# Rotated keys of the cross attention: two of four blocks multiplied in pieces among the self attention's last exponentials, GpSimd adding and halving them, query blocks ahead of the last keys

## The chip, the cores and the metric

The kernel runs on one core of one Trainium2 chip. A core has TensorE (PE, matrix products; its weight loads are shown as PEld), VectorE (DVE), ScalarE (ACT), GpSimd (POOL) and SyncE (SP, which issues DMAs). They run side by side, each through its own queue in the order of the program, and wait for each other on semaphores. The metric is the device time of one execution in microseconds (us), lower is better. TensorE's clock has two levels, 2.4 and 1.2 GHz; the profile shows the granted share as 1.00 and 0.50.

## The reference, cut to what matters

A decoder of two layers on `x` (4, 512, 256) with a context (4, 1024, 256): windowed attention, attention with latents, a ternary feed forward, self attention, cross attention with rotary positions, and a routed feed forward of eight experts. Each is added to `x` behind a layer norm. The change is in the cross attention, whose keys and values come from the raw context:

```python
q = proj(query, Wq, bq, Lq)          # 16 heads of 16; query = layernorm(x), 512 rows
k = proj(key, Wk, bk, Lk)            # key = ctx_1024, 1024 rows
v = proj(value, Wv, bv, Lk)
q = apply_rope(q, q_cos, q_sin)      # (x1 c - x2 s, x1 s + x2 c)
k = apply_rope(k, k_cos, k_sin)
scores = jnp.einsum('bhqd,bhkd->bhqk', q, k) * scale
attn = jax.nn.softmax(scores, axis=-1)
out = jnp.einsum('bhqk,bhkd->bhqd', attn, v)
```

## The kernel before, in words

The kernel goes through the four batch elements one after the other, and in each through the six stages. A product of float32 quality is made of float16 halves: each operand is a high and a low half, and `product` adds high x high, high x low and low x high (L574, L575, L576) over the two chunks of the 256 contracted rows. A product of 128 x 512 thus takes six matrix instructions.

*Rotation.* Six blocks of 128 rows (eight heads) by 512 columns (tokens) are rotated, numbered j: j = 0 to 3 are the keys (feature half j // 2, token half j % 2), j = 4 and 5 the queries. `rope_product(b, j)` makes two products for a block, one with the weights and one with weights whose halves of a head are swapped (s_ = 0, 1). `rotate(b, j)` on VectorE adds the biases and multiplies by the tables of cosines and sines (L1841, two instructions of about 0.74 us). The two results are added (L500 on GpSimd for j < 4, L1849 on VectorE for the queries), ScalarE makes the high half (L1352) and VectorE the low half (L1855). Blocks j = 0 and 1 are multiplied in the tail of the self attention, the others at the beginning of the cross attention, the queries last, for they need the norm of `x`.

*Selection.* `select_k` and `select_q` (L953) spread four heads of a block to rows that start at multiples of 64, by products with a table of zeros and ones; ScalarE copies them (L1365, L1370; the first query tile by VectorE, L1900). There are eight such tiles (p_ = 0 to 7).

*Attention* (`attend`, m_ = 0 for self, 1 for cross). First every score is made once with queries on the rows, in *slots* a = 0, 1, ... (L865, two instructions), and VectorE takes the negated maxima (L1793); a slot reads two of the banks 0 to 3. Four groups of four heads each get their shift (L875, L1807, L1808), which a DMA puts beside the queries. Then the scores are made again with keys on the rows (L897, two per *half step*), ScalarE takes the exponentials (L1340), and `weigh` multiplies them with the values (L911). After a group's last, ScalarE copies the output (L1331), TensorE transposes it (L921), VectorE divides (L1824, L1826). Self attention has 32 slots and 16 steps of two half steps, numbered 0 to 31; the slots run ahead of the steps and end at half step 19. In the first 13 (self) or 21 (cross) slots nothing of the steps runs yet, and `between_self` and `between_cross` put selections and value products (`cross_value`) between the slots.

*Tail.* After the last step: the last L921, `rope_product(b, 0)`, the transpose of the divided output (L628), `rope_product(b, 1)`, ScalarE's and VectorE's halves of it (L1185, L1542), the output projection (L583 to L587, then L574 to L576 of 256 columns), and its additions to `x` with the statistics of the next norm (L1885, L1463). Then the cross attention begins: variance (L1477), reciprocal root on GpSimd (L550), normalised rows (L1483), their transposes (L601) and halves (L1187, L1544). `keep_warm(n, bank)` (L594) issues n products without use.

The order of all this is written out by hand on every engine; on TensorE the lines of `cross_attention(b)` are the blocks j = 2 and 3, transposes, `keep_warm(8, 2)`, blocks 4 and 5, the first selections, `attend(b, 1)`.

## Time and profile before

| | |
|---|---|
| median of 3 runs | 2313.86 us (2306.58 to 2318.06) |
| the profiled execution | 2310.29 us, its span 2308.5 us |
| TensorE busy (matrix products) | 2029.1 us, 88% |
| VectorE | 1771.6 us, 77% |
| ScalarE | 1340.6 us, 58% |
| GpSimd | 205.1 us, 9% |
| chain that ended last | PE 52%, DVE 27%, DMA 8%, issue 6%, ACT 5% |
| mean granted clock of TensorE | 0.978 |

A batch takes about 565 us. The stretch of the change in the first one lies between 409 and 471 us from the start of the span. "Busy" of TensorE counts the modelled end of each product, so what tells of its pace is the distance of starts. A row of the timeline gives the start and length of a group in us, the engine, the line, what it writes and reads, and in brackets how long the engine was idle before it and what ended that.

### The profile page before, as it was taken

To read this page: it belongs to the slowest core of one execution; us is meant where nothing else is said; L and a number is where in the kernel's file an instruction comes from. 1 tells how busy PE (TensorE), PEld (TensorE's weight loads), DVE (VectorE), ACT (ScalarE), POOL (GpSimd) and SP (SyncE) were. 2 spreads that over 40 slices of the span, in tenths; PEclk is the share of its full clock that TensorE was granted. 3 is DMA by queue.
4 is the path that set the end of the run, shared out by engine and by line. 5 is a ranking of instruction groups with operands and counts; after the bars stand their busy time and mean duration, and the time that the engine had idled before them with its cause. 6 is when DMAs were issued, how large, how long until landed. Compare 5 with 4: busy or idle time off the path is not lost.

```text
span 2308.5 us, 43343 instructions
## 1 busy us (share of the span) xinstructions
PE 2029.1 (88%) x18074; PEld 1142.4 (49%) x18074; DVE 1771.6 (77%) x2755; ACT 1340.6 (58%) x1993; POOL 205.1 (9%) x211
## 2 busy tenths in 40 slices
PE   2899978988989996998899998798998999779898
PEld 1566743323656763242466666333255776433235
DVE  7787878695778867779587786769958888786956
ACT  3566636577356654748636664474844666355682
POOL 2000001141000000114000000101500000011220
PEclk9999989999999998999999999899999999999999
DMA  6276720010047670002006775001001766300100
GB/s 253 44 124 118 130 44 1 1 74 29 19 73 123 125 122 19 2 1 93 11 19 106 120 122 113 0 2 69 25 10 36 124 124 120 75 1 1 74 2 10
DMA packets 417315, 147.68 MB, mean 64 GB/s; under 512 B 404440, under 2 KB 412768, under 8 KB 416224
## 3 DMA queue, kind: packets, MB, share of 16 engines
q1 hardware_dynamic: 416544, 142.82, 30.1%
q8 instruction: 142, 2.33, 0.4%
q0 software_dynamic: 576, 2.10, 0.3%
q14 instruction: 53, 0.43, 0.1%
HBM read 41.86 MB, written 2.10 MB: 19 GB/s over the span
## 4 chain that ended last, share of the span: by engine, by line
PE 52%; DVE 27%; DMA 8%; issue 6%; ACT 5%; POOL 1%; SPq 1%; POOLq 0%; DVEq 0%; ACTq 0%
DVE nmx L1793 10%; PE ps L574 10%; PE ps L576 9%; PE ps L575 9%; DMA arena<-arena 7%; PE ps L911 4%; PE ps L736 3%; DVE arena L1632 3%; PE ps L953 2%; PE ps L897 2%; PE ps L730 2%; PE ps L731 2%; PE ps L594 2%; PE ps L865 2%; DVE arena L1737 1%
## 5 line engine op out<-in xcount | busy, mean ns | idle before, releaser
L1793 DVE TENSOR_REDUCE nmx<-ps 128x2 f32<-128x1024 f32 x384 | 444.0, 1217 | 22.1 <-PE ps L865 20.4
L1340 ACT ACTIVATE arena<-ps 128x512 f32<-128x512 f32 x768 | 405.3, 602 | 55.0 <-PE ps L897 50.2
L574 PE MATMUL ps<-arena 128*128 128x512 f16 (+1 forms) x800 | 273.4, 342 | 3.5 <-DVE arena L1933 2.7
L575 PE MATMUL ps<-arena 128*128 128x512 f16 (+1 forms) x800 | 273.2, 341 | 0.0
L576 PE MATMUL ps<-arena 128*128 128x512 f16 (+1 forms) x800 | 273.0, 341 | 0.0
L1619 DVE TENSOR_SCALAR_CACHE_REDUCE ps<-ps 128x1536 f32<-128x1536 f32 x128 | 225.8, 1764 | 54.1 <-PE ps L576 53.5
L911 PE MATMUL ps<-arena 128*17 128x256 f32 x3072 | 237.8, 385 | 0.0
L1632 DVE SCALAR_TENSOR_TENSOR arena<-arena,rs 128x1536 f16<-128x1536 f32 x128 | 231.5, 1809 | 4.2 <-ACT arena L1245 4.2
L1245 ACT ACTIVATE arena<-arena,rs 128x1536 f16<-128x1536 f32 x128 | 200.8, 1568 | 40.1 <-DVE rs L1625 40.1
L1238 ACT ACTIVATE arena<-ps,nm 128x1536 f32<-128x1536 f32 x128 | 197.1, 1540 | 19.5 <-DVE ps L1619 19.5
L730 PE MATMUL ps<-arena 128*128 128x128 f16 x1536 | 185.3, 219 | 3.3 <-DMA arena<-arena 3.1
L731 PE MATMUL ps<-arena 128*128 128x128 f16 x1536 | 185.3, 219 | 0.0
L897 PE MATMUL ps<-arena 64*128 64x512 f16 x768 | 172.6, 387 | 14.3 <-DMA arena<-arena 10.2
L865 PE MATMUL ps<-arena 64*128 64x512 f16 x768 | 148.7, 385 | 17.7 <-DVE nmx L1793 9.4
L574 PE MATMUL ps<-wh,arena 128*128 128x128 f16 (+2 forms) x856 | 154.9, 223 | 6.5 <-DVE arena L1555 6.5
L730 PEld LDWEIGHTS ps<-arena 128*128 128x128 f16 x1536 | 150.2, 98 | 11.9 <-DMA arena<-arena 4.4
L575 PE MATMUL ps<-wl,arena 128*128 128x128 f16 (+2 forms) x856 | 154.6, 223 | 0.0
L576 PE MATMUL ps<-wh,arena 128*128 128x128 f16 (+2 forms) x856 | 154.5, 223 | 0.0
L731 PEld LDWEIGHTS ps<-arena 128*128 128x128 f16 x1536 | 150.3, 98 | 7.5
L550 POOL TENSOR_TENSOR rstd<-ve,col 128x4 f32<-128x4 f32 x20 | 20.2, 1010 | 1408.4 <-DVE ve L1477 1238.5
L897 PEld LDWEIGHTS ps<-arena 64*128 64x128 f16 x768 | 48.1, 92 | 181.3 <-ACT arena L1340 136.3
L736 PE MATMUL ps<-arena 128*128 128x128 f16 x1536 | 108.3, 221 | 29.2 <-DMA arena<-arena 29.1
(254 smaller groups left out, 3855.8 us busy)
## 6 DMA issues: line engine op xcount, KB each, us to landing
arena<-in_experts SPq DMA_DIRECT2D x4, 3840.0 KB, 11.7
arena<-in_weights SPq DMA_DIRECT2D x8, 929.0 KB, 12.6
arena<-in_ctx SPq DMA_DIRECT2D x4, 1024.0 KB, 5.3
arena<-arena SPq DMA_TRANSPOSE x256, 3.7
arena<-in_ctx_t SPq DMA_DIRECT2D x4, 1024.0 KB, 4.8
arena<-in_ternary SPq DMA_DIRECT2D x2, 1024.0 KB, 5.9
y<-in_x POOLq DMA_DIRECT2D x4, 512.0 KB, 4.2
x<-in_x SPq DMA_DIRECT2D x4, 512.0 KB, 3.8
```

The costliest lines, as they stand in the source:

```text
L574: mm(out_, lh, rh, start=(k == 0), stop=False)
L575: mm(out_, lh, rl_, start=False, stop=False)
L576: last = mm(out_, ll, rh, start=False, stop=(k == n - 1))
L730: mm(d_, vh[:, kt, :], ph[:, kt, :], start=(kt == 0), stop=False)
L731: mm(d_, vl[:, kt, :], ph[:, kt, :], start=False, stop=False)
L897: mm(ps[:, 4 + n % 3, :], ks[rows, 2 * g_ + pp, P * kt:P * kt + P], qs[rows, 2 * g_ + pp, :], start=True, stop=True).then_inc(b_mm.sem, 1)
L911: mm(ps[32 * j:32 * j + VW, 7, cols], v17[:, kt, 4 * g_ + j, :], pr_[:, (4 * t + j) % RING, cols], start=(kt + half == 0), stop=(kt == mod ...
L1245: A(xq[i % 2][0], xp[:, i % 2, :], ACT.Copy, scale=rs[:, i:i + 1]).then_inc(s_hi.sem, 1)
L1340: A(pr_[:, n % RING, :], ps[:, 4 + n % 3, :], ACT.Exp).then_inc(b_exp.sem, 1)
L1619: TS_(s_, s_, -XS, None, ALU.mult, ALU.min, accum_out=nm[:, i:i + 1]).then_inc(s_max.sem, 1)
L1632: STT(xq[i % 2][1], xp[:, i % 2, :], rs[:, i:i + 1], xq[i % 2][0], ALU.mult, ALU.subtract).then_inc(s_lo.sem, 1)
L1793: V.tensor_reduce(nmx[:, g_ % 2, ch, :, pp, i], ps[:, 2 * (z % 2):2 * (z % 2) + 2, :], AX.X, ALU.max, negate=True)\
```

## The change

Each block is now handled in parts: `rope_part(b, j, s_)` is one of its two products, and `rotate(b, j, s_)` one of the two instructions on VectorE. `RP_PARTS` is the order.

- Blocks 0 and 1 (four products, 24 instructions) leave the tail. `early_rope` issues them from half step 22 of the self attention on: two instructions in front of each `weigh` up to half step 31, then one in front of each of the last four. They write banks 1 and 3. VectorE rotates block 0 in steps 12 and 13 and block 1 ahead of the last output.
- GpSimd adds and makes both halves of all key blocks and of the second query block (`turned`); ScalarE's and VectorE's halves of them go. The first query block keeps VectorE for the sum and the low half, ScalarE for the high half.
- The cross attention begins with one product of block 2, the first selection of keys, the other product of block 2; then the transposes of the normed rows, both products of block 4, and the first products of blocks 3 and 5. The second products of 5 and 3 come behind the slots 0 and 1, as do their rotations. `keep_warm(8, 2)` goes.
- Value products 0 to 3 stood behind the slots 1, 2, 5, 6 and stand behind 2, 4, 5, 6.
- `rt` gets a third room (8 KB to 12 KB per partition).

TensorE, self attention of the first batch, from the L897 pair of half step 28. Before (L897 scores, L921 transposes of the output, L911 weighing, L628 transposes of `y`):

```order
L897 MATMUL ps<-arena 128x512 x2
L921 MATMUL ps<-ident,arena 128x128 x4
L911 MATMUL ps<-arena 17x256 x4
L897 MATMUL ps<-arena 128x512 x2
L911 MATMUL ps<-arena 17x256 x4
L628 MATMUL ps<-ident,y 128x128 x4
L897 MATMUL ps<-arena 128x512 x2
```

Of the change (L927, L951, L941, L658 are the same four, L1103 the key products):

```order
L927 MATMUL ps<-arena 128x512 x2
L951 MATMUL ps<-ident,arena 128x128 x4
L1103 MATMUL ps<-arena,wh 128x512 x2
L941 MATMUL ps<-arena 17x256 x4
L927 MATMUL ps<-arena 128x512 x2
L1103 MATMUL ps<-arena,wl 128x512
L1103 MATMUL ps<-arena,wh 128x512
L941 MATMUL ps<-arena 17x256 x4
L658 MATMUL ps<-ident,y 128x128 x4
L927 MATMUL ps<-arena 128x512 x2
```

Two key products stand ahead of each weighing. At the end of the same stage, before (12 key products, L574 to L576, stand between L921 and L628):

```order
L911 MATMUL ps<-arena 17x256 x20
L921 MATMUL ps<-ident,arena 128x128 x4
L574 MATMUL ps<-arena,wh 128x512
L575 MATMUL ps<-arena,wh 128x512
L576 MATMUL ps<-arena,wl 128x512
```

Of the change (L613 is the first product of the output projection):

```order
L941 MATMUL ps<-arena 17x256 x4
L1103 MATMUL ps<-arena,wl 128x512
L941 MATMUL ps<-arena 17x256 x4
L1103 MATMUL ps<-arena,wh 128x512
L941 MATMUL ps<-arena 17x256 x4
L1103 MATMUL ps<-arena,wh 128x512
L941 MATMUL ps<-arena 17x256 x4
L1103 MATMUL ps<-arena,wl 128x512
L941 MATMUL ps<-arena 17x256 x4
L951 MATMUL ps<-ident,arena 128x128 x4
L658 MATMUL ps<-ident,y 128x128 x4
L613 MATMUL ps<-wh,yT_hi 128x256
```

The last five weighings are parted by four single products, and the tail has none. VectorE from the halves of the normed rows to the first slots of the cross attention, before (L1841 rotations, L1855 low halves, L1849 sums, L1900 first query tile, L1793 maxima):

```order
L1544 TENSOR_TENSOR yT_lo<-ps,yT_hi 128x512 x2
L1841 SCALAR_TENSOR_TENSOR arena<-ps,col,rope_k 128x512 x2
L1855 TENSOR_TENSOR arena<-arena 128x512
L1841 SCALAR_TENSOR_TENSOR arena<-ps,col,rope_q 128x512 x2
L1849 TENSOR_TENSOR arena<-arena 128x512
L1855 TENSOR_TENSOR arena<-arena 128x512
L1841 SCALAR_TENSOR_TENSOR arena<-ps,col,rope_q 128x512 x2
L1855 TENSOR_TENSOR arena<-arena 128x512
L1849 TENSOR_TENSOR arena<-arena 128x512
L1900 TENSOR_SCALAR arena<-ps 128x512
L1793 TENSOR_REDUCE nmx<-ps 128x2
L1855 TENSOR_TENSOR arena<-arena 128x512
```

Of the change (L1594, L1890, L1897, L1901, L1951 and L1843 for L1544, L1841, L1849, L1855, L1900 and L1793):

```order
L1594 TENSOR_TENSOR yT_lo<-ps,yT_hi 128x512 x2
L1890 SCALAR_TENSOR_TENSOR arena<-ps,col,rope_q 128x512 x2
L1897 TENSOR_TENSOR arena<-arena 128x512
L1890 SCALAR_TENSOR_TENSOR arena<-ps,col,rope_k 128x512
L1901 TENSOR_TENSOR arena<-arena 128x512
L1890 SCALAR_TENSOR_TENSOR arena<-ps,col,rope_q 128x512
L1951 TENSOR_SCALAR arena<-ps 128x512
L1843 TENSOR_REDUCE nmx<-ps 128x2
L1890 SCALAR_TENSOR_TENSOR arena<-ps,col,rope_q 128x512
L1843 TENSOR_REDUCE nmx<-ps 128x2
L1890 SCALAR_TENSOR_TENSOR arena<-ps,col,rope_k 128x512
L1843 TENSOR_REDUCE nmx<-ps 128x2 x14
```

One low half of six is left, and two rotations have moved behind the slots.

The diff, cut to its core:

```diff
+        RP_PARTS = ((0, 0), (0, 1), (1, 0), (1, 1), (2, 0), (2, 1), (4, 0), (4, 1), (3, 0), (5, 0), (5, 1), (3, 1))
+        RP_BANK = dict(zip(RP_PARTS, (1, 3, 1, 3, 6, 7, 4, 5, 6, 7, 7, 7)))
+        RP_ROOM = (0, 1, 0, 1, 2, 0)
+        RP_POOL = (0, 1, 2, 5, 3)
+        EARLY_ROPE = 22
...
-        CROSS_SELECT, CROSS_VALUE = (3, 7, 11, 12, 14, 15, 16), (1, 2, 5, 6, 9, 10, 18, 19)
+        CROSS_SELECT, CROSS_VALUE = (3, 7, 11, 12, 14, 15, 16), (2, 4, 5, 6, 9, 10, 18, 19)
...
+            def turned(b, j):
+
+
+                n, r_ = RP_POOL.index(j), rt[:, RP_ROOM[j]]
+                pool.wait_ge(rp_mul.sem, rp_mul.at(b, rp_upto(j, 1)))
+                nc.gpsimd.tensor_tensor(r_[:, 0, :], r_[:, 0, :], r_[:, 1, :], ALU.add).then_inc(rp_sum.sem, 1)
+                if j == 0:
+                    pool.wait_ge(sel_mm.sem, sel_mm.at(b, LH))
+                pool.wait_ge(rp_sum.sem, rp_sum.at(b, n + 1))
+                nc.gpsimd.tensor_copy(rp_dest(j, 0), r_[:, 0, :]).then_inc(rp_hi.sem, 1)
+                pool.wait_ge(rp_hi.sem, rp_hi.at(b, n + 1))
+                nc.gpsimd.tensor_tensor(rp_dest(j, 1), r_[:, 0, :], rp_dest(j, 0), ALU.subtract).then_inc(rp_lo.sem, 1)
...
                 for k in range(5):
                     if k == 3:
-                        add_rotated(b, 0)
+                        turned(b, 0)
+                        turned(b, 1)
                     pool.wait_ge(var_ready.sem, var_ready.at(b, k + 1))
...
                     if k == 3:
-                        for j in range(1, 4):
-                            add_rotated(b, j)
+                        for j in RP_POOL[2:]:
+                            turned(b, j)
...
                     pe.wait_ge(lv_hi.sem, lv_hi.at(b, 2 + i // 2))
+                elif i == 0:
+                    pe.wait_ge(rp_mul.sem, rp_mul.at(b, 12))
...
 
             def between_cross(b, a):
 
-                if a in CROSS_SELECT:
+                if a == 0:
+                    rope_part(b, 5, 1)
+                elif a == 1:
+                    rope_part(b, 3, 1)
...
                             output_slot(b, mode, mode.output_after(2 * t + half))
+                        if m_ == 0 and 2 * t + half == EARLY_ROPE:
+                            pe.wait_ge(cr_lo.sem, cr_lo.at(b, DC))
+                            pe.wait_ge(sl_free.sem, sl_free.at(b, mode.slot0 + mode.z_shift[GROUPS - 1] + 1))
+                        if m_ == 0 and 2 * t + half >= EARLY_ROPE:
+                            early_rope(b, 2 * (2 * t + half - EARLY_ROPE), 2)
                         if t >= 2:
...
                 for t in range(mode.steps - 2, mode.steps):
                     for half in range(2):
+                        if m_ == 0:
+                            early_rope(b, 20 + 2 * (t - mode.steps + 2) + half, 1)
                         weigh(b, mode, t, half)
                 output_slot(b, mode, GROUPS - 1)
+                pe.wait_ge(y_ready.sem, y_ready.at(b, Y_FIRST[3 + 2 * m_] + 1))
                 if m_ == 0:
-                    pe.wait_ge(cr_lo.sem, cr_lo.at(b, DC))
-                    rope_product(b, 0)
-                pe.wait_ge(y_ready.sem, y_ready.at(b, Y_FIRST[3 + 2 * m_] + 1))
+                    pe.wait_ge(rp_mul.sem, rp_mul.at(b, 4))
                 transpose_chunk(1, 1)
-                if m_ == 0:
-                    rope_product(b, 1)
...
+            def rope_part(b, j, s_, first=0, n=3 * DC):
+
+
+                at = RP_PARTS.index((j, s_))
+                bank, m = RP_BANK[j, s_], rp_source(j)
+                if first == 0:
+                    if at in (2, 3):
+                        pe.wait_ge(rp_mul.sem, rp_mul.at(b, at - 1))
+                    elif at >= 8:
+                        pe.wait_ge(rp_mul.sem, rp_mul.at(b, {8: 5, 9: 6, 10: 10, 11: 11}[at]))
+                name = (("ck", "cks"), ("cq", "cqs"))[j // 4][s_]
+                src = [both(yT, slice(None), c) if j >= 4 else both(crT, slice(None), c, slice(512 * (j % 2), 512 * (j % 2) + 512))
+                       for c in range(DC)]
+                pairs = [(W(name, c, P * m, P), src[c]) for c in range(DC)]
+                if (j, s_) == (4, 0):
+                    last = first_product(b, 4, ps[:, bank, :], pairs, False)
+                else:
+                    for k in range(first, first + n):
+                        (lh, ll), (rh, rl_) = pairs[k // 3]
+                        last = mm(ps[:, bank, :], ll if k % 3 == 2 else lh, rl_ if k % 3 == 1 else rh,
+                                  start=(k == 0), stop=(k == 3 * DC - 1))
+                if first + n == 3 * DC:
+                    last.then_inc(rp_mm.sem, 1)
+
+            def early_rope(b, k, n):
+
+
+                for at in range(k, k + n):
+                    rope_part(b, *RP_PARTS[at // 6], at % 6, 1)
 
             def cross_attention(b):
-                for j in range(2, 6):
-                    if j == 4:
-                        transpose_y(b, 4)
-                        keep_warm(8, 2)
-                    rope_product(b, j)
+                rope_part(b, 2, 0)
+                select_k(b, 1, 0)
+                rope_part(b, 2, 1)
+                transpose_y(b, 4)
+                pe.wait_ge(k_st.sem, k_st.at(b, LH // 2 + 1))
+                for j, s_ in ((4, 0), (4, 1), (3, 0), (5, 0)):
+                    rope_part(b, j, s_)
                 pe.wait_ge(lx_added.sem, lx_added.at(b, NT))
-                select_k(b, 1, 0)
                 select_q(b, 1, 0)
                 attend(b, 1)
...
             def cross_attention(b):
+                stacked_k(b, 1, 0)
                 split_hi(b, 4, yT)
-                for j in range(2, 5):
-                    rotated_hi(b, j)
-                stacked_k(b, 1, 0)
-                rotated_hi(b, 5)
+                first_q_hi(b)
                 for p_ in range(1, 8):
                     if p_ < 4:
                         values_hi(b, 1 + p_, p_ - 1, 7)
...
+            def rotate(b, j, s_):
+
+
+                n = rp_upto(j, s_)
+                dve.wait_ge(rp_mm.sem, rp_mm.at(b, n))
+                if s_ == 0 and j in (2, 3, 5):
+                    dve.wait_ge(rp_lo.sem, rp_lo.at(b, {2: 1, 3: 2, 5: 3}[j]))
+                m, t0 = rp_source(j), 512 * (j % 2)
...
+                name = (("cbk", "cbks"), ("cbq", "cbqs"))[j // 4][s_]
+                STT(rt[:, RP_ROOM[j], s_, :], ps[:, RP_BANK[j, s_], :], C(name, m), tab[:, s_, :], ALU.add, ALU.mult)\
+                    .then_inc(rp_mul.sem, 1)
...
                     slots(b, mode, a, a + 1)
                     if m_ == 0 and a < 2:
                         self_lo(b, 2 + a)
-                    elif m_ == 1 and a == 0:
-                        rotated_lo(b, 5)
...
+                        rotate(b, 0, 1)
                 add_rows(("sbo", "cbo")[m_])
+                if m_ == 0:
+                    rotate(b, 1, 0)
+                    rotate(b, 1, 1)
                 outputs(b, mode, GROUPS - 1)
                 split_lo(b, 3 + 2 * m_, yT, bias=("sbv", "cbv")[m_])
-                if m_ == 0:
-                    rotate(b, 0)
...
 
             def cross_attention(b):
                 moments(b, 3, x, NT)
-                rotate(b, 1)
-                rotated_lo(b, 0)
+                rotate(b, 2, 0)
                 normalise(b, 3, x, y)
-                rotated_lo(b, 1)
-                rotate(b, 2)
+                rotate(b, 2, 1)
                 split_lo(b, 4, yT)
-                rotate(b, 3)
-                rotated_lo(b, 2)
-                rotate(b, 4)
-                rotate_sum(b, 4)
-                rotated_lo(b, 3)
-                rotate(b, 5)
-                rotated_lo(b, 4)
-                rotate_sum(b, 5)
+                rotate(b, 4, 0)
+                rotate(b, 4, 1)
+                first_q_sum(b)
+                rotate(b, 3, 0)
+                first_q_lo(b)
+                rotate(b, 5, 0)
                 first_q(b, 1)
```

## Rows read from the trace of the kernel before

**Rows 1.** Stretches: their ends, length, busy (count) by engine, granted clock, DMA, GB/s.
```profile
427.31:436.01 8.70, 8.70 (x57) 5.60 (x58) 4.94 (x11) 1.32 (x2) 1.27 (x1) 1.00 0.00 1
454.10:459.74 5.64, 5.64 (x28) 2.39 (x26) 5.22 (x6) 1.39 (x2) 0.00 (x0) 0.70 0.00 0
```

**Rows 2.** Timeline of TensorE in the last exponentials: start, us, group [idle before].
```profile
412.53 0.58 PE L897 MATMUL ps<-arena 64*128 64x512 f16 x2
...
415.01 0.39 PE L897 MATMUL ps<-arena 64*128 64x512 f16 x2 [0.37 <-DMA arena<-arena]
...
418.92 0.49 PE L897 MATMUL ps<-arena 64*128 64x512 f16 x2
...
420.10 0.63 PE L921 MATMUL ps<-ident,arena 128*128 128x128 f32 x4 [0.68 <-ACT arena L1331]
...
421.21 0.39 PE L897 MATMUL ps<-arena 64*128 64x512 f16 x2
421.53 0.63 PE L911 MATMUL ps<-arena 128*17 128x256 f32 x8
422.09 0.66 PE L628 MATMUL ps<-ident,y 128*128 128x128 f32 x4
422.68 0.39 PE L897 MATMUL ps<-arena 64*128 64x512 f16 x2
...
424.07 2.35 PE L911 MATMUL ps<-arena 128*17 128x256 f32 x40
427.31 0.63 PE L921 MATMUL ps<-ident,arena 128*128 128x128 f32 x4 [0.89 <-ACT arena L1331]
```

**Rows 3.** Timeline of ScalarE, an exponential and the halves of the normed rows.
```profile
421.63 1.09 ACT L1340 ACTIVATE arena<-ps 128x512 f32<-128x512 f32 x2 [0.70 <-PE ps L897]
...
442.84 1.08 ACT L1187 ACTIVATE yT_hi<-ps 128x512 f16<-128x512 f32 x2 [1.24 <-PE ps L601]
```

**Rows 4.** Timeline of VectorE from the norm to the maxima.
```profile
437.74 0.17 DVE L1477 TENSOR_SCALAR ve<-mv 128x4 f32<-128x4 f32 x1
...
439.74 2.32 DVE L1483 TENSOR_SCALAR y<-x,mv,rstd 128x256 f32<-128x256 f32 x4
...
443.90 1.27 DVE L1544 TENSOR_TENSOR yT_lo<-ps,yT_hi 128x512 f16<-128x512 f32 x2
...
452.82 0.69 DVE L1900 TENSOR_SCALAR arena<-ps 128x512 f16<-128x512 f32 x1
...
459.74 10.42 DVE L1793 TENSOR_REDUCE nmx<-ps 128x2 f32<-128x1024 f32 x9 [0.41 <-PE ps L865]
```

**Rows 5.** Timeline of TensorE from the transposes to slot 0 of the cross attention.
```profile
442.75 1.89 PE L594 MATMUL ps<-wh,ident 128*128 128x512 f16 x8
444.48 0.38 PE L583 MATMUL ps<-yT_hi,wh 128*128 128x512 f16 x1
...
452.18 0.60 PE L953 MATMUL ps<-arena,sel 128*128 128x512 f16 x2 [1.49 <-DVE arena L1855]
453.66 0.61 PE L865 MATMUL ps<-arena 64*128 64x512 f16 x4 [0.88 <-DVE arena L1900]
```

**Rows 6.** Stretches: the cross attention's tail in batches 0 and 1 (columns of Rows 1).
```profile
560.88:567.79 6.91, 5.44 (x33) 3.66 (x34) 3.73 (x9) 0.69 (x1) 0.00 (x0) 0.75 0.00 0
1122.05:1127.89 5.84, 4.09 (x33) 3.07 (x34) 3.63 (x9) 0.69 (x1) 0.00 (x0) 1.00 0.01 3
```

**Rows 7.** GpSimd by line: shapes, count, busy us, mean ns, idle before.
```profile
L521 POOL TENSOR_TENSOR arena<-arena 128x512 f16<-128x512 f32 x64 | 74.2, 1159 | 5.1
L519 POOL CAST arena<-arena 128x512 f16<-128x512 f32 x64 | 39.1, 611 | 184.2 <-DMA arena<-in_experts 180.4
L500 POOL TENSOR_TENSOR arena<-arena 128x512 f32<-128x512 f32 x16 | 23.3, 1456 | 253.5 <-DVE arena L1841 253.5
L550 POOL TENSOR_TENSOR rstd<-ve,col 128x4 f32<-128x4 f32 x20 | 20.2, 1010 | 1408.4 <-DVE ve L1477 1238.5 <-DVE ve L1475 170.0
```

80 lines of the change are left out of this document (29 added, 51 removed).

## The prediction

> **What bounds the kernel now.** I read the page first: its chain of waits is 52% TensorE and 27% VectorE, so neither engine alone sets the end, and each stage has to be read for itself. Then the timeline, engine by engine, of one batch from the self attention's last exponentials (409 us) to the cross attention's twelfth score slot (470 us). The other three batches repeat it within 0.3 us a step, so I work out one batch and take it four times.
>
> Three stretches matter. *Until 427.3 us* ScalarE's exponentials and TensorE share the pace. The reader is to see that TensorE is nearly full: a half step (L897 pair, then L911) that waits for nothing goes L897 421.21, L911 421.53, next shape 422.09, thus 0.32 + 0.56 = 0.88 us, while the six half steps from 412.53 to 418.92 take 6.39, or 1.06 each, of which one holds a DMA wait of 0.37 [rows 2]. So there is about 0.1 to 0.2 us of room in a half step. ScalarE's own waits are for TensorE [rows 3]. *427.3 to 436.0 us*: the tail. TensorE is 100% busy [rows 1], but with the 24 key products (two blocks), which stand in front of the second transpose (L628) and of the output projection. *436.0 to 454.1 us*: VectorE is almost without a gap from the norm's variance (L1477, 437.74) to the first stacked query (L1900, 452.82), and TensorE waits 1.49 us for a low half before the query's selection [rows 4, 5]. From slot 0 (454.10) VectorE's maxima set the pace, 1.15 us each: (10.42 - 1.23) / 8 [rows 4].
>
> **The change part by part.** All steps are for one batch.
>
> (a) *24 products go into the exponentials.* One 128x512 product is 0.216 us: the eight of L594 take 444.48 - 442.75 = 1.73 [rows 5]. A pair of them in a half step costs 0.43 plus a change of tile shape. That change has a price: the L897 pair streams in 0.216, and L911 follows after 0.32, so 0.10. From the other side, four transposes (L628, 4 x 0.109 = 0.44) put between L911 and L897 cost 1.47 - 0.88 = 0.59, so 0.15 [rows 2]. I take 0.10, the more frequent row: a half step becomes 0.88 + 0.53 = 1.41 us, bound by TensorE, and the room in it is used up. The starts then go:
> half step 22 412.53 as before; 24 at 415.35 (before 415.01, the DMA wait of 0.37 is filled); 28 at 420.99 (before 418.92: +2.07). The output's transposes L921 wait for ScalarE's copy, which absorbs 0.3: +1.76 [rows 2]. Half step 29: +0.43 (no new shape after the transposes), so +2.2; 30: +2.7; 31: +3.25; its L911 +3.6, since before it took 0.52 and has only 0.2 of room. Then four single products between the last five L911 groups, which before ran without a gap (40 in 2.35 us, no wait inside) [rows 2]: 0.216 + 2 x 0.10 each, 1.7 together. The last L921 starts at +5.3, 432.6 us. Bounds of this term: +3.5 if a change of shape were free, +6.0 with 0.15 for each.
>
> The Trainium skill states a rule against this edit, in "TensorEngine Tiling (Array Packing)", Key Properties: changing the tiling mode, not just the tile, drains TensorE. The trace agrees, with 0.10 to 0.15 us a change; by the rule as measured the term is 5.3, without it 3.5.
>
> (b) *The tail without key products.* The cross attention's own tail is the same code without them: 5.84 us from L921 to the end of the projection with the full clock (batch 1), 6.91 with the clock at 0.75 on average (batch 0), against 8.70 here [rows 1, 6]. So -2.86: the projection ends at +2.4 (half level of the clock: +3.5). The two rotations of VectorE lie before the last output and wait for nothing else (products done about 1.4 us before L921).
>
> (c) *The norm.* The variance shifts by +2.4. Before, VectorE began to normalise at 439.74, 1.83 us after the variance's end (437.91), because two rotations and a low half stood between; in the cross tail's norm the wait is GpSimd's power alone, 1.01 and the signals [rows 7]. Now one half of a rotation (0.74) lies in that wait, so 0.7 comes back: +1.7, last y at 443.8 instead of 442.06 [rows 4]. GpSimd's queue now holds two whole blocks ahead of the power: add 1.46, high half 0.61, low half 1.16 (the expert split's rows stand for both), 3.2 us a block [rows 7]. The second is released by the rotation at about 432.1 and done by 435.5, 5 us before the variance: no cost.
>
> (d) *Queries.* Before, the high half starts 0.78 us after the last y, since the transposes queue behind a key block; now about 0.4. High halves 1.08, then VectorE's low halves end at 446.0 instead of 445.17 [rows 3, 4]. keep_warm (1.73 us) goes, but TensorE must wait for the low halves anyway: the first query product ends at +0.5. Behind it: four products of 1.3, with rotate, rotate, sum, ScalarE's half, low half, select, first_q on VectorE: 0.7 each. VectorE loses four low halves and a sum of 0.68 in this stretch, and two halves of rotation move behind the slots. I get first_q at 451.2 instead of 452.82, and the first score at 452.1 instead of 453.7: -1.6 [rows 4, 5].
>
> (e) *The first slots.* Two halves of rotation now stand between the maxima, and each is a loop: TensorE 1.3 us of products behind the slot, VectorE waits, 0.7 us rotation, next slot; the second product waits for the bank of the first. Slot 0 at 452.5, rotation 454.1, slot 1 at 454.8, rotation 456.3, slot 2 at 457.0, slot 3 at 458.2 and slot 4 at 459.9, against 459.74 before: +0.2; the lead of 1.6 is spent. Value product 1 now stands behind slot 4, so ScalarE's copy holds product 2 (behind slot 5) until 461.35, and the selection before slot 8 pushes slot 8 to 465.3; before it was 459.74 + 4 x 1.15 = 464.3. So +1.0 [rows 4]. After that VectorE's pace, then the chain of selections, carry any shift on one for one. GpSimd's last blocks end at about 461, and are wanted at 469: hidden.
>
> Sum: 5.3 - 2.9 - 0.7 - 1.2 - 2.1 + 1.8 + 0.8 = +1.0 us a batch, +4 us for four. (-1.2 is y to first query product, -2.1 from there to the first score.)
>
> (f) *The clock.* Before, slots 0 to 3 run with 0.70 of the clock [rows 1], behind 1.49 and 0.88 us without work [rows 5], and VectorE waits 0.41 for TensorE before slot 4 [rows 4]; one batch of the four stays at full clock. With products in the gaps this should mostly go: -0.41 x 3 = -1.2. The new self tail has the waits of the cross tail, which in two batches of four met the half level, at 6.91 - 5.84 = 1.07 [rows 6]: 2 x 1.07 = +2.1.
>
> Total 2310.3 (profiled execution; span 2308.5, 1.8 around it) + 4 + 0.9 = 2315 us. That execution is 0.15% under the median 2313.86, inside the runs' spread of 2306.6 to 2318.1, so I leave the prediction at 2315.
>
> **The rivals.**
> *The products are hidden after all.* If the waits in the exponentials took all 24 (0.37 for the DMA, 0.68 and 0.89 for ScalarE's copies), (a) would be 0 and each batch 4.3 us shorter: 2315 - 21 = 2294. For it: ScalarE, not TensorE, is said to bound such a stage, and its rows are long chains without a gap. Against it: the waits add up to 1.9 us, the product comes behind L921, not into its wait, and 0.88 of 1.06 us is TensorE's own.
> *The clock falls.* keep_warm is gone, and TensorE has short waits from 440 to 446 us and again at 450 to 452. If the half level (1.2 GHz) meets the query products and the first slots in most batches, TensorE loses half of a low stretch of 3.4 us in each, 1.7, as the L574 products of 454.10 to 459.74 show [rows 1]; in all four batches with both places, and the tail low in all: 2315 + 4 x 3.4 + 2.1 = 2331. It decides the sign from about 1.9 us a batch on. For it: two of four tails of the same form. Against: in the new stretch TensorE works over half of the time, where before the low rows it had 0.43 us of it between two waits of 2.37 together [rows 5].
> The Trainium skill's "TensorE: Matmul & The Clock Gate", Part 4, says that transposes do not count as TensorE work in the same way, so the eight at 442 to 444 us may not hold the clock; no row here parts this. By it this rival would be likelier.
> *GpSimd slows VectorE.* Each batch adds 5 x 1.8 us of GpSimd copies and subtracts next to VectorE's work. If VectorE's SBUF operations ran longer by a third in the 14 us from 436 to 452, that would be 2 us a batch: 2323. Against: GpSimd's additions are what stretches beside VectorE (1.27 to 1.65 us), VectorE's low halves stay at 0.68 [rows 7].
>
> **How the numbers follow.** Forecast 0.72, hidden 0.10, clock 0.13, GpSimd 0.05. What can be told from no change is 0.5%, 11.6 us: 2.9 us a batch. The forecast's own bounds: per batch -0.8 (shape changes free) to +1.7, and clock 0 to +4 in all, 2307 to 2321, with the spread between executions 2305 to 2325. For 8 in 10 I go to 2303 and 2326. Faster by over 0.5%: the hidden case and a tail of the forecast, 0.13. Slower: clock, a part of GpSimd, a tail, 0.15. Same 0.72.
>
> **What would show it.** (a) L897 starts 1.4 us apart from half step 22 on, ScalarE with gaps of 0.3 to 0.4, and the last L921 about 20 us after half step 22's L897 (before 14.8). 16 us would mean hidden. (b) 5.8 to 6.9 us from it to the projection's end. (c) normalise 1.1 us after the variance. (d) first_q 12.8 us after the projection's end, not 16.8. (e) slot 4 about 7.4 us after slot 0 (before 5.64), with VectorE waiting for TensorE before both rotations. (f) granted clock 1.00 in slots 0 to 3 in most batches. The prediction is wrong if the batch, slot 8 to slot 8, moves by more than 2 us either way.

## The result, and the profile after

The changed kernel takes 2320.84 us (median of 17 runs, 2312.93 to 2330.58), the kernel before in the same comparison 2309.03 us. The ratio is 1.0046, 95% interval 1.0032 to 1.0060; the medians alone give 1.0051. That is a loss of half a per cent at the edge of what was called "same", and inside the range of 2303 to 2326, but 6 us above the forecast of 2315. One of the 17 runs of the kernel before took 2970.40 us, the others 2304.83 to 2318.06; the ratio leaves that one out. The profiled executions have spans of 2317.5 and 2308.5 us.

The marks below are starts, each counted from the start of half step 22's score pair (L897 before, L927 after) in the same batch, and the table gives after minus before. So a number is what the change has cost by then in that batch.

| start of | forecast | batch 0 | 1 | 2 | 3 |
|---|---|---|---|---|---|
| half step 24 | +0.3 | +1.14 | +0.90 | +0.22 | +0.23 |
| half step 31 | +3.25 | +4.19 | +3.94 | +3.27 | +3.27 |
| last output transposes (L951) | +5.3 | +6.32 | +6.06 | +5.40 | +5.40 |
| variance (L1527) | +2.4 | +4.71 | +3.17 | +4.49 | +2.51 |
| end of the last y (L1533) | +1.7 | +3.08 | +1.54 | +2.86 | +0.87 |
| first stacked query (L1951) | -1.6 | +0.04 | -1.50 | +0.01 | -2.16 |
| slot 4 (L1843) | +0.2 | +1.85 | +0.30 | +2.26 | -0.11 |
| slot 8 | +1.0 | +2.67 | +1.12 | +3.08 | +0.70 |

From slot 8 the shift stays to slot 20. The four sum to 7.6 us; the spans differ by 9.0. The cross attention's tails add 1.8 us: from their last output transposes to the variance they take 9.56, 8.43, 7.58 and 8.40 us after the change and 8.64, 7.58, 7.58 and 8.40 before, with code that is the same.

That small remainder hides larger ones. Outside the marks the code has not changed, and yet its five stretches (to the first half step 22, from each slot 8 to the next half step 22, and from the last slot 8 to the end) take -4.2, +6.4, -3.9, +2.9 and +0.2 us more than before. In the first two the granted clock is 0.98 for 0.97 and 0.96 for 0.98. They nearly cancel in these two executions, which is chance.

The products in the exponentials, TensorE's timeline of batch 1 (start, us, group), answering to [rows 2]:

```profile
979.40 0.39 PE L927 MATMUL ps<-arena 64*128 64x512 f16 x2
979.72 0.39 PE L1103 MATMUL ps<-arena,wl 128*128 128x512 f16 x1
979.95 0.38 PE L1103 MATMUL ps<-arena,wh 128*128 128x512 f16 x1
980.26 0.63 PE L941 MATMUL ps<-arena 128*17 128x256 f32 x8
980.82 0.39 PE L927 MATMUL ps<-arena 64*128 64x512 f16 x2
...
998.28 0.63 PE L951 MATMUL ps<-ident,arena 128*128 128x128 f32 x4 [0.89 <-ACT arena L1388]
999.79 0.66 PE L658 MATMUL ps<-ident,y 128*128 128x128 f32 x4 [0.88 <-DVE y L1876]
```

A half step is 980.82 - 979.40 = 1.42 us, where 1.41 was forecast. A pair of products takes 0.54 of it: 0.43 of streaming and 0.11 for the changes of tile shape. The two long waits of the tail are 0.89 before L951 and 0.88 before L658; no product lies in either. In batch 0 a transfer is late ahead of half step 24 (wait 0.53 us):

```profile
410.82 0.63 PE L941 MATMUL ps<-arena 128*17 128x256 f32 x8
411.98 0.39 PE L927 MATMUL ps<-arena 64*128 64x512 f16 x2 [0.53 <-DMA arena<-arena]
```

The stretches of the tail and of slots 0 to 4, answering to [rows 1, 6] (length, busy of PE, PEld, DVE, ACT, POOL, granted clock, DMA, GB/s):

```profile
429.45:436.76 7.31, 5.87 (x34) 3.84 (x35) 3.95 (x10) 0.69 (x1) 2.46 (x3) 0.77 0.00 1
449.96:457.41 7.45, 6.40 (x34) 2.41 (x33) 6.22 (x6) 0.00 (x0) 4.95 (x6) 1.00 0.01 2
998.28:1004.32 6.04, 4.31 (x34) 3.16 (x35) 3.85 (x9) 0.69 (x1) 2.46 (x3) 1.00 0.02 4
1559.97:1567.97 8.00, 6.56 (x33) 4.25 (x34) 4.03 (x10) 0.69 (x1) 2.46 (x3) 0.64 0.00 0
2124.68:2130.72 6.04, 4.31 (x34) 3.16 (x35) 3.85 (x9) 0.69 (x1) 2.46 (x3) 1.00 0.01 3
```

Lines 1, 3, 4 and 5 go from the last output transposes to the last addition (L1936); line 2 is slots 0 to 4. The same emptied tail takes 6.04 us where the granted clock is 1.00 and 7.31 or 8.00 where it falls to its half level (1.2 GHz) for a part. The row of the slots is one of four with the same 7.45 and a clock of 1.00.

VectorE in batch 1, from the variance to slot 4, answering to [rows 4]:

```profile
1005.84 0.17 DVE L1527 TENSOR_SCALAR ve<-mv 128x4 f32<-128x4 f32 x1
1005.92 0.75 DVE L1890 SCALAR_TENSOR_TENSOR arena<-ps,col,rope_k 128x512 f32<-128x512 f32 x1
1007.14 1.38 DVE L1533 TENSOR_SCALAR y<-x,mv,rstd 128x256 f32<-128x256 f32 x4 [0.47 <-POOL rstd L580]
1008.44 0.75 DVE L1890 SCALAR_TENSOR_TENSOR arena<-ps,col,rope_k 128x512 f32<-128x512 f32 x1
1009.57 1.29 DVE L1594 TENSOR_TENSOR yT_lo<-ps,yT_hi 128x512 f16<-128x512 f32 x2 [0.39 <-ACT yT_hi L1244]
...
1017.52 1.23 DVE L1843 TENSOR_REDUCE nmx<-ps 128x2 f32<-128x1024 f32 x1 [0.59 <-PE ps L895]
1018.91 0.75 DVE L1890 SCALAR_TENSOR_TENSOR arena<-ps,col,rope_q 128x512 f32<-128x512 f32 x1 [0.16 <-PE ps L1103]
1019.58 1.21 DVE L1843 TENSOR_REDUCE nmx<-ps 128x2 f32<-128x1024 f32 x1
1021.23 0.75 DVE L1890 SCALAR_TENSOR_TENSOR arena<-ps,col,rope_k 128x512 f32<-128x512 f32 x1 [0.43 <-PE ps L1103]
1021.89 2.58 DVE L1843 TENSOR_REDUCE nmx<-ps 128x2 f32<-128x1024 f32 x2
1024.97 2.35 DVE L1843 TENSOR_REDUCE nmx<-ps 128x2 f32<-128x1024 f32 x2 [0.50 <-PE ps L895]
```

The normalisation is down from 2.32 to 1.38 us, and VectorE waits for TensorE ahead of both rotations and ahead of slot 4.

### The profile page after: what moved, and what is told of

The parts are those of the page before. It is cut to its first block, busy times and chain, and to the rows that moved or that the text cites. A ratio compares the mean times of both kernels' runs of the same rounds, so it can differ in the third digit from the quotient of the medians.

```text
span 2317.5 us, 43278 instructions
## 1 busy us (share of the span) xinstructions
PE 2036.4 (88%) x18042; PEld 1134.0 (49%) x18042; DVE 1758.9 (76%) x2731; ACT 1330.3 (57%) x1973; POOL 246.1 (11%) x255
## 4 chain that ended last, share of the span: by engine, by line
PE 55%; DVE 24%; DMA 8%; ACT 6%; issue 6%; POOL 1%; SPq 0%; POOLq 0%; DVEq 0%; ACTq 0%
PE ps L604 9%; PE ps L606 9%; PE ps L605 9%; DVE nmx L1843 8%; DMA arena<-arena 7%; PE ps L941 4%; PE ps L766 3%; PE ps L985 3%; DVE arena L1682 3%; PE ps L927 2%; PE ps L1103 2%; PE ps L895 2%; PE ps L760 2%; PE ps L761 2%; PE ps L624 2%
## 5 line engine op out<-in xcount | busy, mean ns | idle before, releaser
L1843 DVE TENSOR_REDUCE nmx<-ps 128x2 f32<-128x1024 f32 x384 | 445.5, 1218 | 27.2 <-PE ps L895 24.8
L941 PE MATMUL ps<-arena 128*17 128x256 f32 x3072 | 242.1, 387 | 0.0
L927 PE MATMUL ps<-arena 64*128 64x512 f16 x768 | 170.4, 390 | 12.4 <-DMA arena<-arena 8.0
L927 PEld LDWEIGHTS ps<-arena 64*128 64x128 f16 x768 | 45.9, 93 | 179.6 <-ACT arena L1397 139.9
```

What stands on the lines that cost most here:

```text
L927: mm(ps[:, 4 + n % 3, :], ks[rows, 2 * g_ + pp, P * kt:P * kt + P], qs[rows, 2 * g_ + pp, :], start=True, stop=True).then_inc(b_mm.sem, 1)
L941: mm(ps[32 * j:32 * j + VW, 7, cols], v17[:, kt, 4 * g_ + j, :], pr_[:, (4 * t + j) % RING, cols], start=(kt + half == 0), stop=(kt == mod ...
L1843: V.tensor_reduce(nmx[:, g_ % 2, ch, :, pp, i], ps[:, 2 * (z % 2):2 * (z % 2) + 2, :], AX.X, ALU.max, negate=True)\
```

## The experiments

Medians and ratios are over alternating rounds with the kernel before on the same chip. The groups of experiments ran on different chips; there the kernel before has medians of 2308.5 to 2309.7 us, and the runs of one kernel spread over 8 us and more. A difference between two experiments' medians is thus good to some 3 us (an estimate); the marks of the profiles are read beside it. "Slot 8" is the last row of the table above for that kernel. Theory after the result: the early products cost what they take plus a change of shape; the rest of the loss is the low clock in the emptied tail and the queue of late products at the slots. The diffs are cut to their core; "..." marks what is left out.

**1. Filling the tail with matmuls of no use.**

```diff
                 output_slot(b, mode, GROUPS - 1)
+                if m_ == 0:
+                    keep_warm(4, 4)
 ...
                 transpose_chunk(1, 1)
+                if m_ == 0:
+                    keep_warm(3, 4)
```

> The changed kernel with seven products without use in the self attention's tail: four behind the last output transposes (L951), three behind the transposes of y (L658), where TensorE waits anyway. Theory (the clock in the emptied tail costs): the granted clock is 1.00 from the last L951 to the projection's end in all four batches, and that stretch is 5.8 to 6.0 us in each, where the changed kernel had 7.45, 5.82, 7.93 and 6.02; 3 to 4 us less in all than the changed kernel, about 2317. Rival (the loss lies only in the exponentials and the first slots): tails of mixed length as before, or the same total within 1 us.

Measured: 2314.10 us (12 runs), ratio 1.0019 [1.0006, 1.0032], 6.7 us below the changed kernel by medians; the two intervals touch. Two of its four tails (the others read the same):

```profile
428.62:434.66 6.04, 5.74 (x41) 3.82 (x42) 3.85 (x9) 0.69 (x1) 2.46 (x3) 1.00 0.00 1
1552.60:1558.64 6.04, 5.74 (x41) 3.82 (x42) 3.85 (x10) 0.69 (x1) 2.47 (x3) 1.00 0.00 0
```

Slot 8 is at +0.80, +1.11, +0.91, +0.70, sum 3.5 against 7.6. The seven matmuls end before the work that they stand in front of is ready, the tail keeps its full-clock length, and the clock stays up. The low clock in this tail is thus a cost of the emptying. Its size is best read from the tails themselves. The same emptied tail without extra matmuls stands in the changed kernel and in experiments 2, 3 and 5, and there the profiled executions lose 3.2, 4.7, 5.6 and 4.3 us in it against 6.04 a batch, more than the forecast's 2.1. The 6.7 us of the medians hold more than the tail: the profiled spans differ by 11.4 us, of which 4.1 lie between the marks and 7.3 in code that is the same.

**2. Twenty of the 24 early products left out.**

```diff
                 for at in range(k, k + n):
-                    rope_part(b, *RP_PARTS[at // 6], at % 6, 1)
+                    if at % 6 == 5:
+                        rope_part(b, *RP_PARTS[at // 6], 5, 1, True)
```

> The changed kernel without 20 of the 24 key products among the exponentials: only the last product of each of the four parts is issued (the keys of blocks 0 and 1 are thus not complete), waits and rotations stay. Theory (the products displace ScalarE's exponentials by what they take): the last L951 starts 15 to 16 us after half step 22's L927 instead of 20.5, slot 8 of the cross attention 4 us a batch earlier against before than in the changed kernel, about 2300 to 2304 us. Rival (the exponentials hide them, the loss is the new order behind the norm and the slots): less than 1 us a batch, above 2315.

This kernel leaves out most of the products for the keys of blocks 0 and 1, so it tells nothing but a time. Measured: 2303.40 us (10 runs), 0.9971 [0.9956, 0.9985]. The last L951 stands at +2.51, +0.94, +0.27 and +0.27; where no transfer disturbs (batches 2 and 3) that is 5.40 - 0.27 = 5.13 us less for 20 products, 0.257 each, changes of shape included. So nothing in the exponentials hid them; the rival by which they vanish in waits is refuted. The other parts of the change, left with four products, gain on the kernel before: slot 8 is at -1.05, -4.02, -2.57 and -2.77.

**3. The same products, six in one place.**

```diff
-                        if m_ == 0 and 2 * t + half >= EARLY_ROPE:
-                            early_rope(b, 2 * (2 * t + half - EARLY_ROPE), 2)
+                        if m_ == 0 and 2 * t + half in EARLY_AT:
+                            early_rope(b, 6 * EARLY_AT.index(2 * t + half), 6)
```

with EARLY_AT = (22, 25, 28, 31), and the four single products between the last L941 groups gone.

> The changed kernel with the same 24 products, but six at a time in half steps 22, 25, 28 and 31, so with 4 instead of 14 places where the tile shape changes. Theory (a change of shape costs 0.1 us): 24 x 0.216 + 0.4 less the waits they fill (0.37, 0.3 and some 0.2 at each place), so the last L951 comes at +4.1 to +4.5 instead of +5.4, about 4 us less in all. Rival (only the products' own time counts, and pieces of two use the room of each half step best): the last L951 at +5.4 or later, the same or slower.

Measured: 2317.01 us (10 runs), 1.0035 [1.0023, 1.0048]. The last L951 stands at +5.06, +5.40, +4.74, +4.74: 0.66 us less than in the changed kernel where no transfer disturbs, with ten places fewer. That is 0.07 us for a place, less than the 0.10 of a shape change that I had taken; the expectation of +4.1 to +4.5 is missed. ScalarE waits 1.28 us for its next scores behind a group of six, 0.33 behind a pair; that this gives back part of the gain is likely and was not tested.

**4. Products in TensorE's waits.** The same 24 products of blocks 0 and 1: three ahead of half step 24 (the wait for the transfer), six in 26, three ahead of the output's transposes of 28 and four ahead of the last ones (ScalarE's copies), five behind these, three behind the transposes of y (L658). Block 1 goes to PSUM banks 5 and 6, and its two rotations on VectorE stand between and behind the two low halves of the tail. Block 0 is rotated one step later, and the first selection of keys stands behind both products of block 2. The diff shows the tail alone.

```diff
+                if m_ == 0:
+                    early_rope(b, 12, 4)
                 output_slot(b, mode, GROUPS - 1)
+                if m_ == 0:
+                    early_rope(b, 16, 5)
                 pe.wait_ge(y_ready.sem, y_ready.at(b, Y_FIRST[3 + 2 * m_] + 1))
 ...
                 transpose_chunk(1, 1)
+                if m_ == 0:
+                    early_rope(b, 21, 3)
```

> The changed kernel with the 24 products put into TensorE's waits: 3 ahead of half step 24 (where it waits for the shift's DMA), 6 in half step 26, 3 ahead of the output transposes of half step 28, 4 ahead of the last ones, 5 behind them, 3 behind the transposes of y; block 1 uses banks 5 and 6 and is rotated between and behind VectorE's low halves; the selection comes behind both products of block 2. Theory: the last L951 at +1.3 to +1.8, the tail 5.8 to 6.0 with the clock at 1.00, slot 8 2 to 3.5 us a batch earlier than in the kernel before: 2298 to 2303 us, a ratio to before of 0.995 to 0.998. Rival (the loss is behind the norm and in the slots): not faster than before, 2312 or more.

Measured: 2303.08 us (12 runs), 0.9973 [0.9960, 0.9987]. TensorE in batch 1:

```profile
984.58 0.60 PE L1110 MATMUL ps<-arena,wh 128*128 128x512 f16 x2
985.02 0.38 PE L1110 MATMUL ps<-arena,wl 128*128 128x512 f16 x1
985.24 0.38 PE L1110 MATMUL ps<-arena,wh 128*128 128x512 f16 x1
985.54 0.63 PE L951 MATMUL ps<-ident,arena 128*128 128x128 f32 x4
986.00 0.38 PE L1110 MATMUL ps<-arena,wh 128*128 128x512 f16 x1
...
987.08 0.65 PE L658 MATMUL ps<-ident,y 128*128 128x128 f32 x4
```

L951 to L658 is 1.54 us, as in the changed kernel (1.51) and with five products more. The last L951 is at +1.7, +2.1, +1.4, +1.4 instead of +5.4 to +6.3, slot 8 at -3.18, -2.87, -3.07, -3.28. With the products in the waits the low clock is gone from all four self tails too. Between two kernels with the same matmuls lie 17.8 us by medians and 20.0 between the marks; 3.2 of the 20.0 are the two low tails of the changed kernel.

**5. The slots.** On the changed kernel: the second product of queries 1 goes to bank 4, two matmuls ahead of the queries' selection and four behind it; that of key block 3 stands behind slot 0 in bank 5; the values start behind slot 1 again. VectorE's order stays. The diff leaves out the banks and the waits.

```diff
+                rope_part(b, 5, 1, 0, 2)
                 pe.wait_ge(lx_added.sem, lx_added.at(b, NT))
                 select_q(b, 1, 0)
+                rope_part(b, 5, 1, 2, 4)
 ...
                 if a == 0:
-                    rope_part(b, 5, 1)
-                elif a == 1:
                     rope_part(b, 3, 1)
```

> The changed kernel with one edit at the score slots: the second products of queries 1 and of key block 3, which it issues behind slots 0 and 1 in bank 7, go ahead. Of the first, two matmuls stand ahead of the queries' selection and four behind it, in bank 4; the second stands behind slot 0, in bank 5; the products of the values start behind slot 1 again, as before the change. VectorE's order is the same: it still rotates both between slots 0, 1 and 2. Theory (the rotations on VectorE are the stretch's work, and the products that come late put waits of 0.16 and 0.43 us ahead of them, and the late value copy one of about 0.4 us behind slot 4): slots 0 to 4 take 7.45 minus 0.6, about 6.8 us, slots 4 to 8 fall from 5.4 to 5.0, and slot 8 stands about 1.0 us a batch earlier against half step 22, 4 us over four batches: about 2316.5 us. Rival (VectorE's own work, four maxima and two rotations of 6.4 us, with slot waits of 0.5 that move along, is all there is): slots 0 to 4 stay at 7.3 to 7.45 and the time stays at 2320. The tail's low clock is as in the changed kernel in either case.

Measured: 2314.81 us (12 runs), 1.0021 [1.0006, 1.0037], 6.0 us below the changed kernel. VectorE in batch 1:

```profile
1019.08 1.23 DVE L1845 TENSOR_REDUCE nmx<-ps 128x2 f32<-128x1024 f32 x1 [0.59 <-PE ps L895]
1020.22 0.74 DVE L1892 SCALAR_TENSOR_TENSOR arena<-ps,col,rope_q 128x512 f32<-128x512 f32 x1
1020.88 1.22 DVE L1845 TENSOR_REDUCE nmx<-ps 128x2 f32<-128x1024 f32 x1
1022.01 0.74 DVE L1892 SCALAR_TENSOR_TENSOR arena<-ps,col,rope_k 128x512 f32<-128x512 f32 x1
1022.67 9.21 DVE L1845 TENSOR_REDUCE nmx<-ps 128x2 f32<-128x1024 f32 x8
```

No wait is left from slot 0 to slot 9. Slots 0 to 4 take 5.85 us instead of 7.45, slots 4 to 8 4.58 instead of 5.41: 2.4 us a batch, more than double the 1.0 that I expected. Slot 8 is at +0.73, -1.31, -0.54 and +0.46; three self tails met the low clock here. I had added up two of the waits that the rows show (0.16 + 0.43) and 0.4 behind slot 4, and had left out the 0.50 ahead of slot 4; and the waits are worth more than they show. From start to start slot 0 to its rotation is 1.39 us with the shown wait of 0.16 and 1.14 without one; slot 2 to slot 4 is 3.08 with a shown 0.50 against 2.30 (two maxima at 1.15, [rows 4]). Back to back, an instruction starts before the one ahead has quite ended; each wait loses that too, some 0.1 to 0.3 us.

**6. Tail and slots together**, on the changed kernel, the edits of experiments 1 and 5.

> The changed kernel with the edits of e1_warm_tail (seven matmuls of no use in the waits of the self attention's tail) and of e7_slots_only (second products ahead of the score slots, values from slot 1 on) together. Theory (the change's loss is two terms, the tail's low clock and the queue of late products at the slots, which lie behind one another; what is left of the change, 24 products in the exponentials against what the emptied tail and the norm give back, comes to nothing or a small gain): slot 8 stands at 0.9 - 2.4 = about -1.5 us against half step 22 of the kernel before, -6 us over four batches, and the time is about 2314.1 - 8 = 2306 us (2303 to 2309), below or at the kernel before. Rival (the early products cost more than the marks show, in clock or in waits elsewhere, and the two repairs overlap): 2311 to 2314, still above the kernel before.

Measured: 2306.77 us (12 runs), 0.9987 [0.9971, 1.0003]. Slot 8 at -1.63, -1.31, -1.51, -1.71. The gains add (6.7 + 6.0 = 12.7; measured 14.1, and 13.7 between the marks), and without the two terms the change is no loss, nor a gain clear of noise: the rival of 2311 or more falls.

**7. Filled waits and slots**, experiment 4 with the edit of 5.

> The kernel e4_fill_waits with the edit of e7_slots_only at the score slots on top: second products of queries 1 and key block 3 ahead, values from slot 1 on. Theory (the terms of tail and slots lie behind one another and add): slots 0 to 4 7.45 to 6.8 us, slot 8 at -4.0 us against half step 22 of the kernel before (e4_fill_waits: -2.9 to -3.3), and 2303 minus 4: about 2299 us, 0.9955 of the kernel before. Rival (what comes earlier at slot 8 is given back by slot 20, where selections and copies set the pace): 2302 to 2303, as e4_fill_waits.

Measured: 2294.54 us (6 runs), 0.9937 [0.9919, 0.9955]. Slot 8 at -5.60, -5.28, -5.49, -5.70, and slot 20 at the same: nothing is given back, and the rival falls. The forecast was too small by 1.5 us a batch, for the same reason as in experiment 5.

**8. The cross attention's tail kept warm**, on experiment 7: experiment 1's edit in the other branch.

```diff
                 if m_ == 0:
                     early_rope(b, 16, 5)
+                else:
+                    keep_warm(4, 4)
```

> The kernel e5_slots with four matmuls of no use behind the cross attention's last output transposes and three behind its transposes of y, as e1_warm_tail has them in the self attention's. Theory (a stretch at the low clock meets the cross attention's tail in some batches, where it took 6.91 us for 5.84 in batch 0 of the kernel before): the tail takes 5.8 us in all batches, 1 to 2 us in all, and 2293 us against 2294.5. Rival (the low stretch comes later anyway, in the experts or the next batch, or the matmuls delay the transposes): 2294 to 2297.

Measured: 2286.96 us (6 runs), 0.9906 [0.9883, 0.9929], the fastest of all by its median; the interval overlaps with experiment 7's. The cross tails of batches 0 and 1, of experiment 7 and then of this one, from the last output transposes to the variance:

```profile
551.52:560.39 8.87, 7.40 (x48) 5.41 (x48) 5.40 (x17) 1.46 (x3) 0.00 (x0) 0.81 0.01 2
1110.38:1119.62 9.24, 7.49 (x48) 5.60 (x48) 5.50 (x16) 1.45 (x3) 0.00 (x0) 0.82 0.01 2
```

```profile
555.70:563.29 7.59, 7.26 (x55) 5.39 (x55) 5.30 (x17) 1.47 (x3) 0.00 (x0) 1.00 0.01 2
1106.80:1114.38 7.58, 7.25 (x55) 5.39 (x55) 5.30 (x16) 1.46 (x3) 0.00 (x0) 1.00 0.01 2
```

All four take 7.58 now. In the two profiles that is 1.29 + 1.66 = 2.9 us; the medians differ by 7.6. The mean granted clock of the profiled runs is 0.980 against 0.976: the rest goes with low stretches elsewhere, in code that did not change. Why there are fewer of them stays open. That the matmuls are what keeps this tail's clock up is not shown by four tails: without them 17 of the 40 cross tails of the other ten profiles have this length, and in experiment 4 all four.

**9. The normalisation without GpSimd beside it.** The kernel before with one wait more:

```diff
                 dve.wait_ge(rstd_ready.sem, rstd_ready.at(b, k + 1))
+                if k == 3:
+                    dve.wait_ge(rp_sum.sem, rp_sum.at(b, 2))
```

> The kernel before with one wait more: VectorE's normalisation of the cross attention's input (L1483, four instructions, 2.32 us) starts only when GpSimd's second addition of rotated keys (L500) has ended, which takes 1.64 us beside it where the addition at 433.87 takes 1.27 us. Theory (the two slow each other when they run side by side): the four instructions take 1.38 us, GpSimd's addition about 1.27 to 1.35, and the last y is no more than 0.5 us later. Rival (the normalisation took 2.32 us for its own sake, for instance where its input lies, and the changed kernel altered that): 2.32 us, the last y 1.4 us later, GpSimd's addition 1.64.

Measured in one profiled run. The tile's view (count, shortest/median/longest in ns), the kernel before first, then the experiment:

```profile
L1483 DVE TENSOR_SCALAR y<-x,mv,rstd x4: 399/400/1353, 439.7 to 441.7; 128x256 f32<-128x256 f32 x4
```

```profile
L1485 DVE TENSOR_SCALAR y<-x,mv,rstd x4: 408/410/415, 437.2 to 438.2; 128x256 f32<-128x256 f32 x4
```

and GpSimd's addition, in the kernel before and in the experiment:

```profile
439.30 1.64 POOL L500 TENSOR_TENSOR arena<-arena 128x512 f32<-128x512 f32 x1 [0.29 <-DVE arena L1841]
```

```profile
435.48 1.64 POOL L500 TENSOR_TENSOR arena<-arena 128x512 f32<-128x512 f32 x1 [0.29 <-DVE arena L1843]
```

In the kernel before only the first of four instructions was long: it was issued at 439.74 and ended at 441.09, just behind the addition's end at 440.94. With the wait all four take 0.41; they start 1.31 us later and the last y ends only 0.37 later. That half of the theory holds. The other half fails: the addition takes 1.64 us without the normalisation beside it too. What is beside it in both kernels is the subtraction ahead (L1855 at 439.14 for 0.68, two inputs in SBUF). The profiles on record settle this. In the kernel before, all eight additions that start 0.15 us behind such a subtraction take 1.64 or 1.65 us, four of them with no normalisation near, and the other eight take 1.27:

```profile
444.06 1.27 POOL L500 TENSOR_TENSOR arena<-arena 128x512 f32<-128x512 f32 x1 [3.12 <-DVE arena L1841]
446.42 0.68 DVE L1855 TENSOR_TENSOR arena<-arena 128x512 f16<-128x512 f32 x1
446.57 1.65 POOL L500 TENSOR_TENSOR arena<-arena 128x512 f32<-128x512 f32 x1 [1.25 <-DVE arena L1841]
```

In the changed kernel 16 of GpSimd's 20 subtractions take 1.16, and the four that start 0.15 us behind VectorE's long addition (L1599, two inputs in SBUF, at 988.80 for 1.22 us in batch 1) take 2.08 or 2.09:

```profile
988.96 2.09 POOL L530 TENSOR_TENSOR arena<-arena 128x512 f16<-128x512 f32 x1
999.73 1.16 POOL L530 TENSOR_TENSOR arena<-arena 128x512 f16<-128x512 f32 x1
```

## Why the prediction was right, and what was mis-sized

The outcome is the forecast's case, and its steps can be read one by one. The total came out closer than its terms: errors of 1 to 4 us cancel in it, as (f) shows, and that is luck. The prediction's own sign of being wrong even appears: from slot 8 to the next slot 8 the changed kernel takes 7.5 us more, 0.8 less and 3.7 more than before, where it named 2 us. By (a) to (e) slot 8 moved 1.9 us a batch against the half step 22 of the same batch (1.0 forecast); the rest is the unchanged code between the batches, which the forecast had held fixed.

(a) *Right.* 1.41 a half step was forecast, 1.42 is there; the last transposes at +5.3, measured +5.40 in batches 2 and 3. In batches 0 and 1 there are 0.9 and 0.7 more. I let the products fill the wait of 0.37 for the transfer. In batch 0 the transfer ends later after the change, and in batch 1 the kernel before had next to no wait there (its half step 24 starts 2.13 us after half step 22, against 2.80 in batches 2 and 3), so there was nothing to fill. The price of 0.10 for changes of tile shape held, with 0.11 here and 0.07 net in experiment 3.

(b) *Right with the full clock*: -2.88 from L951 to the last addition in batches 1 and 3, -2.86 forecast. The term that failed in size is the clock's, in (f).

(c) *Too small.* I gave back 0.7 between variance and last y; it was 1.63 in every batch. I had read 2.32 us for the normalisation as its own duration, while 0.95 of it was GpSimd's addition (experiment 9), and the change removes that too. This is 3.7 us of gain over four batches that the forecast did not have.

(d) *Right*: from last y to first stacked query -3.3 forecast, -3.0 measured. (e) *Right for the changed kernel*: slots 0 to 4 7.4 forecast, 7.45 measured in all four batches; slots 4 to 8 +0.8, measured +0.82. But the kernel before took 5.63, 5.65, 5.20 and 5.20 for slots 0 to 4, and I had read batch 0 alone. Experiment 5 shows that this was a cost of the order, not of the work.

(f) *The mis-sized step.* The terms, summed over four batches, and what lies between the marks in their place:

| term | forecast | measured |
|---|---|---|
| (a) products in the exponentials | +21.2 | +23.2 |
| (b) tail, with its clock | -9.3 | -8.3 |
| (c) norm | -2.8 | -6.5 |
| (d) last y to slot 0 | -13.2 | -12.2 |
| (e) slots 0 to 8 | +10.4 | +11.4 |
| (f) clock at the slots | -1.2 | in (e) |
| clock in the cross tails | 0 | +1.8 |

The clock terms stood at +0.9. The -1.2 was counted twice: 7.4 us for slots 0 to 4 was already the pace of a full clock. It was misread, too: the wait of 0.41 ahead of slot 4 stood in two batches, not in three. In the self tail I took 1.07 us for a low stretch, twice. It did meet two tails of four, but cost 7.31 - 6.04 = 1.27 and 8.00 - 6.04 = 1.96, since it lay over the projection, where TensorE sets the pace. And I priced no other place, while the cross tails lost 1.8 us in this pair of executions. Together that is 1.2 + 1.1 + 1.8 = 4.1 us too little, which the norm's 3.7 us nearly covers. What (a) missed (2.0, of which 1.6 are the transfers of batches 0 and 1) and an optimistic (d) and (e) (1.0 each) make up the difference of 4 between the spans (+9.0 for +4.9), but for 0.3 in code that is the same. The 3.2 us of the self tails are at the low end: experiments 2, 3 and 5 lost 4.7, 5.6 and 4.3 there.

*The rivals.* "Hidden" is refuted by experiment 2. "The clock falls" named the right mechanism and the wrong place: at the first slots the clock is 1.00 in all four batches, as (f) had it. "GpSimd slows VectorE" is wrong in sign here: the two do hold each other up, but VectorE's normalisation paid it in the kernel before. In the changed kernel, from the tail to slot 12, no instruction of VectorE takes over 3% longer than its like before; there it is GpSimd that waits (2.08 for 1.16 us), and its next instruction comes 6.7 us later anyway.

## What to carry to other kernels

Work that is moved forward to empty a tail should go into waits that the timeline names, not where its data is first ready: the same 24 products leave the variance 2.5 us late when spread over the half steps (batch 3), and 1.5 us early in the waits (experiment 4, which also moved two rotations), both at the full clock. An emptied stretch of short waits has to be priced at both levels of the clock, with the row where TensorE sets its pace. Before a difference of two profiles is shared out, compare the stretches that did not change: here they differ by up to 6.4 us. And where two engines hand work to each other, compare starts, with and without a wait: the shown waits gave 1.09 us for what was worth 1.6.

## What the runs showed of the hardware

VectorE's TENSOR_SCALAR from SBUF to SBUF (128x256, f32) and GpSimd's addition (128x512, f32) did not run side by side: the first instruction took 1.353 instead of 0.40 us and ended 0.15 us behind the addition, the next three were normal. The Trainium skill, "SBUF — State Buffer", "SBUF: two separate sides", describes the port pair that the two engines share as an exclusive lock, held for the whole instruction by whichever starts first, for VectorE's two-port modes and for its instructions with two SBUF inputs. The trace agrees, in the 1.353 us. It agrees with the other order too: GpSimd's addition took 1.64 for 1.27 us, and its subtraction 2.08 for 1.16, behind a VectorE instruction with two SBUF inputs that had started 0.15 us before; both ended 0.15 us short of one own duration after its end (1.12 and 1.02 us).

GpSimd, in the changed kernel, takes 1.27 us for an addition of 128x512 in f32, 0.61 for the conversion to f16 and 1.16 for the subtraction into f16:

```profile
1009.26 1.27 POOL L524 TENSOR_TENSOR arena<-arena 128x512 f32<-128x512 f32 x1 [2.16 <-DVE arena L1890]
1010.59 0.61 POOL L528 CAST arena<-arena 128x512 f16<-128x512 f32 x1
1011.28 1.16 POOL L530 TENSOR_TENSOR arena<-arena 128x512 f16<-128x512 f32 x1
```

Seven matmuls in waits of under a microsecond were enough to hold the clock in the self attention's tail. With matmuls of no use (experiments 1 and 6) or key products (4, 7 and 8) in its waits, 20 of 20 tails take 6.03 to 6.07 us to the last addition; with the waits left empty (the changed kernel, experiments 2, 3 and 5) 4 of 16 take 6.03 or 6.04 us, and the others 7.01 to 8.00.
